# Two state-space blocks of a decoder: scans of one state over two sequences in place of one state over four, most input products on GpSimd, outputs summed by transposes

## The reference, cut to what matters

```python
x = einsum(in_proj_w, ctx); u = silu(causal_conv4(x) + conv_b)      # 256 channels
dt_lo, B, C = split(x_proj_w @ u)                                   # 8, 16, 16 rows
delta = softplus(dt_proj_w @ dt_lo + dt_proj_b);  A = -exp(A_log)   # 16 states
state = state * exp(delta * A) + (delta * u) * B                    # for each position
y = sum over the 16 states of state * C;  y = (y + D * u) * silu(z) # z: the activations x
x = layernorm(x + y)
```

## Time and profile before

| | us |
|---|---|
| median of three runs | 2671.76 |
| lowest and highest | 2666.47, 2681.22 |
| the profiled execution's own time | 2666.48 |
| its span | 2664.5 |
| span outside: own time less span | 2.0 |

### The profile page before, as it was taken

How to read it: one execution, slowest core, us unless ns; L and a number is a source line. 1 busy time by engine, 2 the same in 40 slices (tenths; PEclk the granted TensorE clock), 3 DMA queues, 4 the chain that set the end, 5 groups by cost and what they waited for, 6 DMA issues and landing times.

```text
span 2664.5 us, 27749 instructions
## 1 busy us (share of the span) xinstructions
PE 1977.8 (74%) x9734; PEld 1251.4 (47%) x9734; DVE 1610.6 (60%) x2456; ACT 786.8 (30%) x1999; POOL 580.7 (22%) x327
## 2 busy tenths in 40 slices
PE   5646668746635776788888864553999999999986
PEld 3522234412222445666666633343566665555743
DVE  4279956879988543555555179998366424444114
ACT  1333302133212025455554011110355314444000
POOL 1314420014501014233332036555000000000000
PEclk9867878768867879888889877876899999999966
DMA  3000020010010210000001100000000100000000
GB/s 102 7 32 0 0 54 3 5 45 0 0 40 1 35 42 2 17 12 12 12 10 50 71 1 0 0 0 0 6 10 10 42 10 13 12 10 21 1 32 16
DMA packets 25727, 48.98 MB, mean 18 GB/s; under 512 B 6262, under 2 KB 19603, under 8 KB 24092
## 3 DMA queue, kind: packets, MB, share of 16 engines
q1 hardware_dynamic: 25644, 47.85, 5.9%
HBM read 42.20 MB, written 1.05 MB: 16 GB/s over the span
## 4 chain that ended last, share of the span: by engine, by line
PE 51%; DVE 37%; ACT 4%; issue 4%; SPq 1%; POOL 1%; DMA 1%; DVEq 0%; ACTq 0%; POOLq 0%
DVE big L795 8%; PE banks L1116 7%; PE banks L1085 7%; PE banks L1125 7%; PE banks L1054 6%; DVE big L1796 5%; PE banks L1108 3%; DVE big L1792 3%; DVE big L495 2%; PE banks L1350 2%; PE banks L417 2%; PE banks L428 2%; DVE big L790 2%; DVE big L776 1%; DVE arena L1172 1%
## 5 line engine op out<-in xcount | busy, mean ns | idle before, releaser
L1191 DVE COPY arena<-banks 128x512 f32<-128x512 f32 x196 | 135.4, 691 | 329.8 <-PE banks L1108 329.5
L218 POOL TENSOR_TENSOR ln_rstd<-ln_var_eps,neg_half 128x2 f32<-128x2 f32 x48 | 36.8, 766 | 1060.8 <-DVE ln_var_eps L206 1060.8
L1085 PE MATMUL banks<-big 128*128 128x256 f32 x784 | 235.6, 413 | 6.0 <-ACT big L1227 4.4
L1116 PE MATMUL banks<-arena,big 128*128 128x256 f32 x784 | 227.7, 414 | 6.3 <-DVE arena L1191 6.3
L1248 ACT ACTIVATE arena<-banks,arena 128x256 f32<-128x256 f32 x392 | 193.0, 499 | 60.8 <-DVE arena L1165 43.0
L795 DVE TENSOR_TENSOR_SCAN big<-big 128x2048 f32<-128x2048 f32 x32 | 204.2, 6380 | 1.1
L707 PE MATMUL banks<-big,ident 128*128 128x512 f32 x288 | 171.3, 749 | 39.2 <-POOL big L868 39.1
L868 POOL TENSOR_TENSOR big<-big 128x2048 f32<-128x2048 f32 x32 | 144.7, 4523 | 252.2 <-DVE big L795 252.2
L1266 ACT ACTIVATE big<-banks 128x256 f32 (+1 forms) x196 | 75.1, 383 | 348.4 <-PE banks L1116 348.4
L1054 PE MATMUL banks<-x_feat,arena 128*128 128x512 f32 x392 | 176.4, 592 | 0.0
L1125 PE MATMUL banks<-arena,big 128*128 128x256 f32 x784 | 174.3, 382 | 1.9 <-ACT big L1266 1.9
(11 more groups left out here) (313 smaller groups left out, 3568.1 us busy)
## 6 DMA issues: line engine op xcount, KB each, us to landing
big<-big SPq DMA_DIRECT2D x32, 64.0 KB, 2.3
arena<-in_L0f_w SPq DMA_DIRECT2D x1, 2048.0 KB, 8.0
arena<-in_L1a_wo SPq DMA_DIRECT2D x1, 2048.0 KB
arena<-in_L1f_gv SPq DMA_DIRECT2D x1, 2048.0 KB
arena<-in_L2a_qk_w SPq DMA_DIRECT2D x1, 2048.0 KB
big<-big SPq DMA_DIRECT2D x64, 32.0 KB
arena<-in_L2x_wo SPq DMA_DIRECT2D x1, 2048.0 KB
arena<-in_L2x_q_w SPq DMA_DIRECT2D x16, 128.0 KB, 2.0
```

The lines of the kernel that those rows point to most:

```text
L1085: last = mm(ps[:, h * SEQ:(h + 1) * SEQ], q[:, b * SEQ + h * P:b * SEQ + (h + 1) * P], k[:, b * SEQ:(b + 1) * SEQ], start=True, stop=not s ...
L1116: last = mm(slot, self.v[:, 2 * b + kc, :], self.probs_t[:, u % 2, kc, :], start=(kc == 0), stop=(kc == 1))
L1191: v.tensor_copy(self.probs_t[:, u % 2].rearrange("p a b -> p (a b)"), B[4 + u % 2][:]).then_inc(self.turn_read, 1)
```

## The change

Both blocks stay where they are and still run alone. (The diff also has code by which an attention block could host such a scan; it is switched off in both kernels' block lists, `hosts` is False and `hosted` is False everywhere.) What changes in each state-space block:

- The loop of 16 turns becomes 32 written-out steps. Step k handles one state (k mod 16) and two of the four sequences (the first two in steps 0 to 15, the other two in steps 16 to 31). Decay, product, scan and output product each cover 128 x 1024 elements.
- The input product of a step is on DVE where k mod 8 is 2, 5 or 7, and on POOL otherwise. For POOL, ACT copies B as well as C to SBUF, 1024 elements in one instruction (`bc`, two buffers).
- The output products are no longer summed by identity matmuls. PE transposes them (8 transposes of 128 x 128 a step) and accumulates them in banks 6 and 7, so that the sum comes out in token order; D * u (made on ACT) is added the same way at the end of each half. ACT copies the sum to `du`, DVE multiplies it with the gate, and the layer norm reads it from SBUF instead of PSUM.
- The gate is no longer computed by the block. The layer norm ahead of it applies Silu as it copies to `x_feat` (`gates=True` for the norms behind blocks 0 and 3), in banks 0 to 3.
- `drive` has two buffers; `decay` and one of them lie where the softplus had its scratch, so POOL clears the decay's first positions only after `du` is made.

The core of the diff:

```diff
+HALVES = 2
+STEPS = HALVES * STATES
+    def driver(self, k):
+        return "dve" if k % 8 in (2, 5, 7) else "pool"
+    def driven(self, eng, k):
+        who = self.driver(k)
+        eng.wait_ge(self.s_driven[who], sum(self.driver(n) == who for n in range(k + 1)))
+    def cols(self, k):
+        half = k // STATES
+        return slice(half * BANK, (half + 1) * BANK)
+    def tensor_spread(self, pe, k):
+        if k == 0:
+            pe.wait_ge(self.s_parts, 2)
+        else:
+            pe.wait_ge(self.s_bc_read, k)
+            if self.driver(k - 1) == "dve":
+                self.driven(pe, k - 1)
+        for n in range(2):
+            last = self.e.nc.tensor.matmul(self.e.bank[4 + n][:], self.pick[0:3 * BC, n * STATES + k % STATES, :], self.parts[0:3 * BC, self.cols(k)], start=True, stop=True)
+        last.then_inc(self.s_bc_psum, 1)
+    def tensor_add(self, pe, k):
+        e = self.e
+        first, last = k % STATES == 0, k % STATES == STATES - 1
...
+        pe.wait_ge(self.s_outed, k + 1)
+        sources = [self.out[:, k % 2]] + ([self.u[:, :, self.cols(k)]] if last else [])
...
+            for t in range(4):
+                for j in range(CH):
+                    at = (t % 2) * D + j * P
+                    ins = e.nc.tensor.matmul(e.bank[6 + t // 2][:, at:at + P], src[:, j, t * P:(t + 1) * P], e.ident[:], is_transpose=True,
+                                             start=(first and at == 0), stop=False, skip_group_check=True)
...
+    def tensor_slot(self, pe, s):
+        if s + 1 < STEPS:
+            self.tensor_spread(pe, s + 1)
+        if s:
+            self.tensor_add(pe, s - 1)
+    def vector_drive(self, dve, k):
+        if self.driver(k) == "dve":
+            dve.wait_ge(self.s_du, 1)
+            dve.wait_ge(self.s_bc_psum, k + 1)
+            if k >= 2:
+                dve.wait_ge(self.s_scanned, k - 1)
+            self.e.nc.vector.tensor_tensor(self.drive[k % 2], self.du[:, :, self.cols(k)], bcast(self.e.bank[4][:], 1, CH), ALU.mult).then_inc(self.s_driven["dve"], 1)
+    def vector_slot(self, dve, s):
+        if s + 1 < STEPS:
+            self.vector_drive(dve, s + 1)
+        dve.wait_ge(self.s_cleared, 1)
+        dve.wait_ge(self.s_decay, s + 1)
+        self.driven(dve, s)
+        if s >= 2:
+            dve.wait_ge(self.s_outed, s - 1)
...
+        self.e.nc.vector.tensor_tensor_scan(flat(self.state[:, s % 2]), flat(self.decay[:, s % 2]), flat(self.drive[s % 2]), 0.0,
+                                            ALU.mult, ALU.add).then_inc(self.s_scanned, 1)
+        for pair in range(4):
+            dve.wait_ge(self.s_y_read, pair // 2 + 1)
...
+            v.tensor_tensor(out, out, e.x_feat[:, :, pair * SEQ:(pair + 1) * SEQ], ALU.mult).then_inc(e.y_ready, 1)
+    def scalar_step(self, act, k):
+        a, n = self.e.nc.scalar.activation, k % STATES
...
+            act.wait_ge(self.s_scanned, k - 1)
+        for j in range(CH):
...
+            last = a(seqs(self.decay[:, k % 2, j, :]), seqs(self.delta[:, j, self.cols(k)]), ACT.Exp, scale=self.a_neg[:, j, n:n + 1])
+        last.then_inc(self.s_decay, 1)
+        act.wait_ge(self.s_bc_psum, k + 1)
+        if k >= 2:
+            act.wait_ge(self.s_outed, k - 1)
+        first = self.driver(k) == "dve"
+        a(self.bc[:, k % 2, first:, :], self.e.banks[:, 4 + first:6, :], ACT.Copy).then_inc(self.s_bc_read, 1)
+    def gpsimd_drive(self, pool, k):
+        if k == 0:
+            pool.wait_ge(self.s_du, 1)
+            self.e.nc.gpsimd.memset(self.decay.rearrange("p k j (b t) -> p (k j b) t", t=SEQ)[:, :, 0:1], 0.0).then_inc(self.s_cleared, 1)
+        if self.driver(k) == "pool":
+            pool.wait_ge(self.s_bc_read, k + 1)
+            if k >= 2:
+                pool.wait_ge(self.s_scanned, k - 1)
+            self.e.nc.gpsimd.tensor_tensor(self.drive[k % 2], self.du[:, :, self.cols(k)], bcast(self.bc[:, k % 2, 0, :], 1, CH), ALU.mult).then_inc(self.s_driven["pool"], 1)
+    def gpsimd_slot(self, pool, s):
+        if s + 1 < STEPS:
+            self.gpsimd_drive(pool, s + 1)
+        pool.wait_ge(self.s_bc_read, s + 1)
+        pool.wait_ge(self.s_scanned, s + 1)
+        if s >= 2:
+            pool.wait_ge(self.s_added, s - 1)
+        self.e.nc.gpsimd.tensor_tensor(self.out[:, s % 2], self.state[:, s % 2], bcast(self.bc[:, s % 2, 1, :], 1, CH), ALU.mult).then_inc(self.s_outed, 1)
```

More of the change, by code:

```diff
@@ L347, in sync, with host, room, first_slots @@
                 sp.dma_start(self.q[row:row + 1, g, :], self.max_rows[8 * j:8 * j + 8, g, :]).then_inc(self.rows_moved, 16)
+    def host(self, beside):
+        self.beside = beside
+    def room(self):
+        return self.stage.rearrange("p s k t -> p (s k t)")
+    def first_slots(self, u):
+        at = u - StateSpace.SOFTPLUS
+        return range(at, at + 1) if self.hosts and at >= 0 else ()
+    def second_slots(self, u):
+        first = self.units - StateSpace.SOFTPLUS
+        upto = lambda n: min(first + n // 3 * 5 + n % 3 * 2, STEPS)
+        return range(upto(u), STEPS if u == self.units - 1 else upto(u + 1)) if self.hosts else ()
+    def slot(self, u):
+        return 4 * (u % self.slots)
     def rows(self, j):
@@ L459, in tensor, with proj_bank, v_bank @@
                 last.then_inc(e.y_ready, 1)
+        if self.hosts:
+            self.beside.tensor_slot(pe, STEPS)
+    def proj_bank(self, blk, s, half):
+        return (0 if blk or self.hosts else 4) + 2 * s + half
+    def v_bank(self, pair):
+        return pair if self.hosts else 4 + pair
     def vector(self, dve):
@@ L640, in __init__ @@
-        self.c_all = [big.take(TOKENS) for _ in range(2)]
-        self.out = [big.take(CH * TOKENS) for _ in range(2)]
+        halves = lambda ap: ap.rearrange("p (k j t) -> p k j t", j=CH, t=BANK)
+        self.decay = halves(work[:, 0:2 * TOKENS])
+        self.drive = [work[:, 2 * TOKENS:3 * TOKENS].rearrange("p (j t) -> p j t", j=CH), drive_1]
+        if not self.hosted:
+            room = big.take(4 * TOKENS)
+        self.state, self.out = halves(room[:, 0:2 * TOKENS]), halves(room[:, 2 * TOKENS:4 * TOKENS])
@@ L694, in tensor @@
-        pe.wait_ge(self.s_dt_act, 4)
-        for q in range(4):
-            nc.tensor.matmul(B[4 + q][:], self.zero_bf[:, 0:P], self.zero_bf, start=True, stop=False, skip_group_check=True)
-        pe.wait_ge(self.s_dbl_read, 2)
-        def spread(row, banks):
-            for half in range(2):
-                last = nc.tensor.matmul(B[banks + half][:], self.pick[0:3 * BC, bass.ds(row, 1), :].rearrange("p a b -> p (a b)"),
-                                        self.parts[0:3 * BC, half * BANK:(half + 1) * BANK], start=True, stop=True)
-            last.then_inc(self.s_bc_psum, 1)
@@ new lines, in scalar_y, with scalar_skip @@
+    def scalar_y(self, act, half):
+        a = self.e.nc.scalar.activation
+        k = (half + 1) * STATES - 1
+        cols = self.cols(k)
+        act.wait_ge(self.s_y_psum, half + 1)
+        self.driven(act, k)
+        self.driven(act, k - 1)
+        a(self.du[:, :, cols], self.e.banks[:, 6:8, :], ACT.Copy).then_inc(self.s_y_read, 1)
+    def scalar_skip(self, act):
+        act.wait_ge(self.s_du, 1)
+        for half in range(2):
+            cols = slice(half * BANK, (half + 1) * BANK)
+            for j in range(CH):
+                last = self.e.nc.scalar.activation(self.u[:, j, cols], self.u[:, j, cols], ACT.Copy, scale=self.small[:, j, TAPS + 2:TAPS + 3])
+            last.then_inc(self.s_skip, 1)
@@ new lines, in scalar_slot, with scalar @@
+    def scalar_slot(self, act, s):
+        if s + 1 < STEPS:
+            self.scalar_step(act, s + 1)
+        if s == 0:
+            self.scalar_skip(act)
+        if s % STATES == 1 and s > STATES:
+            self.scalar_y(act, s // STATES - 1)
+    def scalar(self, act):
+        if not self.hosted:
+            self.wait_start(act)
+            self.scalar_in(act)
+            self.scalar_u(act)
+            self.scalar_dt(act)
+            self.scalar_step(act, 0)
+            for s in range(STEPS):
+                self.scalar_slot(act, s)
+            self.scalar_y(act, 1)
```

436 lines of the change are left out of this document (237 added, 199 removed).

## The result

The changed kernel takes 2727.26 us, the median of four runs (2722.82 to 2739.72), against 2673.11 of the kernel before in the same comparison: ratio 1.0205, 95% interval 1.017 to 1.0241. It is slower, by 54 us with an interval of 45 to 64.

A forecast was written before the change was run, and what follows sets the result against it. Time shared by DVE's scan and POOL was taken as the bound. Per block, loop +57.4, start +1.6, end -4.3 make 54.7 us, 109 for both; 2666.5 becomes 2776, as a median 2780, range 2732 to 2812.

The forecast's parts named there:

- The exclusion, and that input products on POOL leave their cover: State-space loop: two-SBUF-input DVE instructions and POOL's take turns; five input products per eight steps add 11.3 us of shared time.
- The gaps: Eight-step round: neither DVE nor POOL works while ACT's copy is awaited, three times 1.2 us, 3.6 us.
- Start and end: Each block before its first scan, +1.6 us, and from last scan to the norm's first add, -4.3 us.
- The shared time of a step, the price of POOL's 1024 elements: Loop: scan 2.21 us and POOL product 2.26, half the 2048-element rows; 47.1 us per eight steps.
- The hand-overs: Loop: changes between scan and POOL add 0.5 us per eight steps, 8 x 0.06.
- short products: Rival: POOL's 1024-element products take 1.92 us, 35 us less for both blocks, 2745 us; chance 0.2.
- More gaps: Rival: scan goes before POOL, two more 1.2 us gaps a round, 2799 us; chance 0.2, shared with dearer products.
- Nothing shared: Rival: half-size scan and POOL instructions overlap, POOL's chain bounds the loop, 2661 us; chance 0.05.

The follow-up runs named there:

- experiment 1: Changed kernel with all 32 input products of a block on DVE, reading B from PSUM: 2652.67 us, ratio 0.9933 to the kernel before.
- experiment 3: Changed kernel, all input products on DVE with B from SBUF, three tries: 2799.03; four buffers and later transposes, 2730.7; ACT also copying first, 2707.34 us.
- experiment 5: Changed kernel with four buffers for B and C instead of two, moved by two floats: 2709.66 us, ratio 1.0143 to the kernel before.
- The shifted kernel: Changed kernel with its two SBUF buffers for B and C moved by two floats: 2775.98 us, ratio 1.039 to the kernel before.
- experiment 6: Changed kernel, all input products on DVE from PSUM, four buffers moved by two floats: 2650.1 us; then PE's transposes one step later too: 2646.08 us.

## Why the prediction was right and wrong

- *The exclusion, and that input products on POOL leave their cover*: right, and shown. It was the ground of the whole sum; with the products back on DVE the loss was gone (experiment 1), with DVE's own product on two SBUF inputs it came back by 1.08 us a step (experiment 3).
- *The gaps*: three a round of 1.20 us, right in place and size; without them a round was 3.4 us shorter (experiment 5).
- *Start and end*: +1.6 and -4.3 predicted, +1.7 or +1.8 and -5.0 or -4.5 measured. Only argued: that the end gains by what was listed; no run took it apart.
- *The shared time of a step, the price of POOL's 1024 elements*: **this term failed.** I weighed rows of 1.89 and 1.94 against 2.35, took half of this product's 4.52, which is 2.26, and gave as the reason that it reads two streams. Measured were 1.99 to 2.00, just at the 2.0 below which I had called the prediction wrong, and the round of 45.6 lies outside the 49 to 53 that the profile should have shown. What sets it is how the two inputs start: 2.34 us if their difference is a multiple of 16 bytes, 1.99 if it leaves 8. The kernel before has the first, the change moved the buffers to the second. 13 products of 0.27 less are 3.5 us of the 5.6 by which the round was too long; 52 a block, 28 us in both. Halving the row was off by only 0.09 (a half in the kernel before takes 2.35); the mistake was to take it over to buffers that begin elsewhere.
- *The hand-overs* were sized wrongly as well. I added 0.5 us a round. In fact an instruction that already queues when the other ends is quicker than one that starts alone: a POOL product ends 1.78 us after the scan instead of 1.99, a scan 2.15 after POOL instead of 2.26. That it has done part of its work ahead would explain this; no run shows it. With products of 1.99 my terms give 8 x 2.21 + 13 x 1.99 + 0.5 + 3.6 = 47.7 us, and 45.6 were measured, so 2.1 us a round, 17 us in the kernel. Added up along the round from 222.68 to 268.27, the 13 products take 24.7 us and not 13 x 1.99 = 25.9, the 8 scans 17.3 and not 8 x 2.21 + 0.5 = 18.2, and the gaps 3.6. The row for it was there: the earlier trace rows has 4.35 us after the other let go, for 4.50 alone, and I read it for the exclusion only.
- With both, the profiled execution's 2776 becomes 2776 - 28 - 17 = 2731, and it took 2731.11. As a median 2780 becomes 2735, inside the range; the median measured is 8 us lower, which lies within the scatter of the runs (2722.82 to 2739.72). The shifted kernel, in which products take 2.34, took 2776: there the price was 0.08 too low, 1.0 us a round, and the hand-overs 2.1 too high, and 51.2 + 1.0 - 2.1 is the measured 50.1. That 2780 comes so near to it is partly luck.
- *Rivals*: "short products" came nearest, 2745 by rows of 1.89 and 1.94, but its reason (one stream) does not fit: these products read two. Nor does the price by starts fit its row of 1.89, which multiplies an array by itself, with no difference between the starts, and is cheap: that price is shown for two different arrays only. "More gaps" did not occur; POOL did go first after a product of its own. "Nothing shared" did not occur.
- *The range* ended at 2732 because I took the whole error to lie in one term at a time. The two errors together give 2735, 3 us above that end, so that the scatter of a few runs was enough to leave the range.

## What to carry to other kernels

Before a product is moved from VectorE to GpSimd to relieve it, look for what covers it now and whether both would have two inputs in SBUF: work that was free under the other engine becomes time that both wait for, and busy shares do not show it. Price an instruction by a row with the same placement of its inputs, not only the same size, and read what a queued instruction takes after its release as well as what it takes alone. A wait that ends before the other engine lets go is no time to be won: taking 0.82 us of it away in each step changed a step by nothing.

## What the runs showed of the hardware

GpSimd's product of two different SBUF arrays takes 4.52 us for 2048 floats a partition and 2.34 for 1024 if the two inputs start a multiple of 16 bytes apart, and 3.81 and 1.99 if the difference leaves 8 bytes; shifts of 0, 4, 8, 12, 16 and 32 floats were dear, 2 and 14 cheap, and moving both inputs alike changed nothing. Two floats of padding made the kernel before faster by 0.84% (0.53 to 1.15). Shifts of 6 or 10 floats and shifts by an odd number were not tried. Why the same place in 16 bytes should be dear stays open.

The Trainium skill, page "SBUF — State Buffer", section "Door 1: The DMA port swizzle", says that SBUF is read in lines of 16 bytes; that the dear shifts above (2.35 us) are multiples of 16 bytes and the cheap ones (2.00) leave 8 agrees with that length, and no run here shows more of it.

The granted clock of TensorE was lower in the changed loops. The busy time by stage, of the kernel before and of the changed one (PE, PEld, DVE, ACT and POOL busy with counts, then the granted clock):

```profile
209.00:355.00 146.00, 100.54 (x197) 36.84 (x197) 139.32 (x48) 50.06 (x63) 72.38 (x16) 0.82 0.00 0
```

```profile
207.30:384.00 176.70, 86.53 (x308) 57.20 (x308) 112.73 (x45) 67.59 (x96) 127.67 (x50) 0.50 0.00 0
```

0.50 is the lower of its two levels, 1.2 GHz; PE was busy for 49% of the time there, and for 69% in the loop before. The steps of experiment 6 show that PE's lateness cost them nothing; in the changed kernel itself this was not tried.
